# Moving the copy of a state's upper part behind the next step's gates in a gated graph network

## The reference

```python
A = (adj != 0)
for l in range(5):
    m = einsum('bnd,de->bne', h, weight[l])
    agg = einsum('bij,bid->bjd', A, m)
    gi = agg @ w_ih.T + b_ih;  gh = h @ w_hh.T + b_hh
    r = sigmoid(i_r + h_r);  z = sigmoid(i_z + h_z)
    n = tanh(i_n + r * h_n)
    h = (1 - z) * n + z * h
```

## Time and profile before

| | |
|---|---|
| median of 3 runs | 735.71 us |
| the profiled execution | 734.84 us |
| its span, first to last instruction | 733.0 us |
| TensorE busy | 684.8 us, 93% |
| VectorE busy | 564.6 us, 77% |
| ScalarE busy | 541.5 us, 74% |
| GpSimd busy | 300.4 us, 41% |
| mean granted TensorE clock | 0.994 |

### The profile page before, as it was taken

One profiled execution on the slowest core, in us unless ns is written; L12 is line 12 of the kernel. 1 busy time (PEld: TensorE's weight loads), 2 busy tenths in 40 slices (PEclk: granted clock), 3 DMA queues, 4 the chain that ended last, 5 costly groups with the idle time before them and its releaser, 6 DMA issues.

```text
span 733.0 us, 12659 instructions
## 1 busy us (share of the span) xinstructions
PE 684.8 (93%) x4226; PEld 587.3 (80%) x4226; DVE 564.6 (77%) x1362; ACT 541.5 (74%) x1167; POOL 300.4 (41%) x427
## 2 busy tenths in 40 slices
PE   3999899989999989989999999989999998989986
PEld 2787788879888779878978868879878887978766
DVE  4689986888978886789988886798886786787334
ACT  5577788668788878667878978657888768647653
POOL 4322435464335443573244534573334225642412
PEclk9999999999999999999999999999999999999999
DMA  6520011200000020410000020110000000110001
GB/s 162 126 80 1 2 30 32 58 1 4 6 4 1 1 61 2 130 44 2 5 7 1 2 61 1 59 59 2 6 6 1 1 1 1 58 58 5 9 1 58
DMA packets 47624, 21.10 MB, mean 29 GB/s; under 512 B 9032, under 2 KB 47560, under 8 KB 47560
## 3 DMA queue, kind: packets, MB, share of 16 engines
q1 hardware_dynamic: 47560, 20.29, 10.3%
HBM read 15.27 MB, written 4.19 MB: 27 GB/s over the span
## 4 chain that ended last, share of the span: by engine, by line
PE 55%; DVE 19%; ACT 14%; issue 6%; POOL 4%; DMA 1%; DVEq 0%; SPq 0%; POOLq 0%; ACTq 0%
PE bank L404 9%; PE bank L406 9%; PE bank L405 9%; PE bank L399 6%; DVE rh L1353 3%; PE bank L390 3%; ACT x_in L704 2%; ACT xn L704 2%; DVE bank L1356 2%; PE bank L592 2%; PE bank L604 2%; PE bank L607 2%; POOL rstd L945 2%; ACT rh L901 2%; PE bank L555 2%
## 5 line engine op out<-in xcount | busy, mean ns | idle before, releaser
L961 POOL TENSOR_TENSOR h_lo<-h,h_hi 128x512 fp32r<-128x512 f32 x64 | 82.6, 1291 | 243.2 <-ACT h_hi L876 243.2
L1353 DVE SCALAR_TENSOR_TENSOR rh<-bank,rh 128x512 f32<-128x512 f32 x80 | 55.0, 688 | 87.0 <-ACT bank L909 86.9
L404 PE MATMUL bank<-h_hi,whh_hi 128*128 128x512 f32 x240 | 105.8, 441 | 12.9 <-DVE rh L1353 11.9
L404 PE MATMUL bank<-g_hi,wc_hi 128*128 128x512 f32 x240 | 102.6, 427 | 0.0
L406 PE MATMUL bank<-h_lo,whh_hi 128*128 128x512 f32 x240 | 95.0, 396 | 0.0
L405 PE MATMUL bank<-h_hi,whh_lo 128*128 128x512 f32 x240 | 94.5, 394 | 0.0
L406 PE MATMUL bank<-g_lo,wc_hi 128*128 128x512 f32 x240 | 94.4, 393 | 0.0
L405 PE MATMUL bank<-g_hi,wc_lo 128*128 128x512 f32 x240 | 93.7, 391 | 0.0
L399 PEld LDWEIGHTS bank<-edge,hn 128*128 128x128 f32 x640 | 83.6, 191 | 8.4 <-DVE edge L1061 2.0
L915 ACT ACTIVATE bank<-bank,bih 128x512 f32<-128x512 f32 x80 | 52.9, 661 | 45.2 <-DVE bank L1356 45.1
L399 PE MATMUL bank<-edge,hn 128*128 128x128 f32 x640 | 84.3, 274 | 1.6 <-DVE edge L1061 1.6
(11 more groups left out here) (168 smaller groups left out, 1668.1 us busy)
## 6 DMA issues: line engine op xcount, KB each, us to landing
x_in<-in_x SPq DMA_DIRECT2D x8, 512.0 KB, 5.4
adj_in<-in_adj SPq DMA_DIRECT2D x8, 512.0 KB, 5.0
x_res<-in_x SPq DMA_DIRECT2D x16, 256.0 KB, 2.8
out_x<-x_res SPq DMA_DIRECT2D x16, 256.0 KB, 2.3
xz<-x_res SPq DMA_DIRECT2D x16, 50.0 KB
w_sb<-in_L_gnn_W SPq DMA_DIRECT2D x1, 640.0 KB, 5.2
w_sb<-in_L_gnn_W SPq DMA_DIRECT2D x5, 128.0 KB, 5.1
rows<-in_adj SPq DMA_DIRECT2D x32, 0.6 KB
```

The source lines that it names most:

```text
L404: nc.tensor.matmul(dst[:], w_hi, m_hi, start=start, stop=False)
L961: nc.gpsimd.tensor_tensor(h_lo[q][:], h[q][:], h_hi[q][:].bitcast(f32), ALU.subtract).then_inc(sem["h_lo_new"], 1)
L1353: nc.vector.scalar_tensor_tensor(rh[:], R_BANK[:], 1.0, rh[:], ALU.add, ALU.mult).then_inc(sem["rh_ready"], 1)
```

## The change

ScalarE's call of `split_new(n - 1)` moves from ahead of the tanh of r to behind the copy to `g_hi`, right ahead of the tanh of n. GpSimd calls `beside(2n)` ahead of `low_half(n - 1)` instead of behind it; `beside(2n + 1)` stays behind. No instruction is added or removed, and the streams of TensorE, VectorE and SyncE are the same.

```diff
@@ scalar
                 beside(2 * n)
-                if n and (n - 1) % STEPS < SPLITS:
-                    split_new(n - 1)
                 act.wait_ge(sem["gates_r"], n + 1)
                 nc.scalar.activation(R_BANK[:], R_BANK[:], ACT.Tanh, bias=brz[:, 0:1], scale=0.5).then_inc(sem["r_ready"], 1)
                 act.wait_ge(sem["gates_z"], n + 1)
                 nc.scalar.activation(gz[n % 2][:], Z_BANK[:], ACT.Tanh, bias=brz[:, 1:2], scale=0.5).then_inc(sem["z_ready"], 1)
                 if n + 1 < ALL:
                     aggregate_hi(n + 1)
+                if n and (n - 1) % STEPS < SPLITS:
+                    split_new(n - 1)
                 act.wait_ge(sem["pre_ready"], n + 1)
@@ gpsimd
             for n in range(ALL + TAIL_STEPS):
+                beside(2 * n)
                 if n and n <= ALL and (n - 1) % STEPS < SPLITS:
                     low_half(n - 1)
-                beside(2 * n)
                 beside(2 * n + 1)
```

## The result

The changed kernel takes 736.7 us, the median of 12 runs (735.12 to 739.14), against 735.36 us for the kernel before in 12 runs. The ratio is 1.0023, with a 95% interval of 1.0012 to 1.0033. The forecast was 0.4% less time; it became 0.2% more. The profiled execution has a span of 734.4 us, 1.4 us more than before.

What follows compares the result with a forecast made beforehand. TensorE, busy 93% of the span, was taken as the bound. +3.0 (round 0) - 5.9 (gains) = -2.9 us took 734.84 to 731.9; the median's 0.87 made 732.8 us. Own range 730 to 735, over all cases 729 to 739.

Steps and rivals of the forecast that it cites:

- (a): Steps 24, 44, 64: gated no longer meets the low half, rh 0.88 us earlier, TensorE idle goes: 2.6 us gained.
- (b): Steps 32 to 34 and 52 to 54: blocks lose 1.0 us, products come 1.4 us earlier; two rounds, 2.8 us.
- (c): Step 74: TensorE's wait of 1.44 us at 606.08 shrinks by 0.5 us.
- The race for zh: Light steps: low half starts 0.04 us before zh, which ends 1.1 us later; the other order's bound is 0.4 us.
- Round 0: Early-step zh delays, a later tanh of n, and normT and adjacency waits: 1.7 + 0.2 + 1.15 = +3.0 us.
- where VectorE is over 1.3 us late it escapes: Steps with VectorE over 1.3 us late: zh was to avoid the low half, taken to end at 2.48 us.
- the clock: TensorE's slow stretch behind idles at 54.57 and 85.98: one more or fewer, 0 in sum, 1.7 us each way.
- Only where VectorE is the last to arrive: Later zh was to cost time only in round 0's early steps, where VectorE arrives last.
- the loop through h: Rival, steps 32 to 36 of each round: h's loop grows up to 1.1 us a step; 741 us, chance 0.20.
- the written signs: If right: gated, mix, blocks never above 0.75 us, hardly any tanh-of-n idle; if wrong: xn of steps 33 to 36 waits longer.
- handed on: Rival: idle removed returns at the next wait for L901, half of 5.9 us goes; 735.7 us, chance 0.28.
- zh did not win its race: Rival: zh starts first in light steps, h loses 0.4 us, round 0 costs 1.5; 731.3 us, chance 0.07.

Runs made afterwards that it cites:

- e2: Kernel before with only GpSimd's even side work moved ahead of the low half, ScalarE's copy left early: 736.4 us, ratio 1.0004.
- e1: Changed kernel with GpSimd's order of before (low half ahead of even side work), ScalarE's copy late: 773.9 us, ratio 1.0503.
- e4: Changed kernel (copy late) with GpSimd's low half one step later, waiting for VectorE's rh: 725.5 us, ratio 0.9846.
- e3: Changed order of ScalarE and GpSimd from step 21 on only, round 0 as in the kernel before: 730.4 us, ratio 0.9917.
- e7: Changed kernel with GpSimd's low half also waiting for g_lo, so it starts just behind zh's start: 727.1 us, ratio 0.9883.
- e5: Kernel before (copy early) with only GpSimd's low half moved, one step later and behind rh: 726.9 us, ratio 0.9877.

## Why the prediction was wrong

**The gains, right.** (a) rh ahead of step 25's products was to come 0.88 us earlier; from step 24 to step 26 the products gain 0.89, 0.88 and 0.83 us in the three rounds. (b) 1.4 us a round was forecast, 1.7 and 1.3 measured. (c) 0.5 forecast, 0.5 measured. Small waits that were not seen took some back. L477 waits 0.3 us for diff in steps 23, 43 and 63; with the 0.28 us gained one step ahead that is some +0.15 us a round. Step 73 adds 0.25. In place of -5.9 the three rounds gave -5.2, less 0.7 lost to a stretch at half clock in step 40 of this execution.

**The race for zh, right.** zh under the low half, its end 0.54 us behind it, the 1.1 us of a light step, and gated, mix and blocks free in steps 24 and 31 to 33: all as written. "GpSimd winning by 0.04 us" is the margin that the trace has in the light steps.

**Round 0, the term that failed.** "Round 0: 1.7 + 0.2 + 1.15 = +3.0 us" came out as +5.9 (0.25 of it the start). The miss lies ahead of the products of step 10, on VectorE's chain from step 3 on:

| term | forecast | measured |
|---|---|---|
| zh of step 3 and b_share | +2.1 | +2.1 |
| blocks no longer caught | -0.95 | -0.9 |
| half clock at 58.49: g_lo of step 5 waits | 0 | +0.85 |
| zh of step 5, less a wait of 0.8 that it fills | 0 | +0.3 |
| zh of step 6 | +1.0 | +1.1 |
| zh of steps 7 and 8 | 0 | +1.0 |
| rowsI | -0.45 | -0.4 |
| rh ahead of the products of step 10 | +1.7 | +4.2 (4.50 less the 0.26 of the start) |

The rows above the last add up to 4.05; a further 0.1 us is a wait ahead of L1356 in step 5, the rest rounding.

A miss of 1.0 us is one that the forecast had ruled out: "where VectorE is over 1.3 us late it escapes". In steps 7 and 8 VectorE is about that late (zh starts 2.50 and 2.30 us after g_hi, against 1.24 in a light step), but so is GpSimd: the low half ends 3.12 and 2.95 us after g_hi starts, and not the 2.48 of the forecast. By GpSimd's own move, put at "Nothing late, I take 0", the norm goes ahead of the low half. Step 8:

```profile
81.23 0.60 ACT L880 ACTIVATE g_hi<-bank 128x512 fp32r<-128x512 f32 x1 [0.45 <-PE bank L399]
...
81.64 1.01 POOL L945 TENSOR_TENSOR rstd<-var_eps,neg_half 128x4 f32<-128x4 f32 x1
...
82.88 1.30 POOL L961 TENSOR_TENSOR h_lo<-h,h_hi 128x512 fp32r<-128x512 f32 x1
83.53 1.19 DVE L1329 SCALAR_TENSOR_TENSOR zh<-gz,h 128x512 f32<-128x512 f32 x1
```

e2 has the same 1.18 us in both steps without the copy's move. e1, without GpSimd's, confirms it for step 7, where zh is back at 0.68 us, but not for step 8: there VectorE is less late, and zh takes 1.37. A miss of nearly the same size is the clock. The idle of 2.46 us at 56.95 was followed by a stretch at the lower level, 1.2 GHz, and the one of 2.36 us at 90.47 was not, where before had it. Granted clock is the number behind the busy times:

```profile
58.49:61.90 3.41, 3.41 (x12) 0.50 0.03 5
90.40:94.90 4.50, 4.43 (x23) 1.00 0.00 0
```

The forecast had said that the stretch could come or go, and put 0. In VectorE's chain it is +0.85. e1 shows the price apart from the rest: it has the same idle at the same place and no such stretch behind it, and its products of step 6 come 1.4 us earlier than those of the changed kernel (1.42 us after before's, not 2.86):

```profile
56.89 0.51 PE L404 MATMUL bank<-h_hi,whh_hi 128*128 128x512 f32 x1 [2.46 <-DVE rh L1353]
...
58.49:61.90 3.41, 3.41 (x23) 1.00 0.03 5
```

The 1.4 us that come back behind step 10 pay for three losses further on: 0.7 in steps 10 to 13 (forecast 0.2, and 0.15 for the adjacency), 0.94 at the two L362, which was right (0.48 and 0.62 us of wait in place of nothing and 0.18), and 1.1 behind step 16. There three VectorE instructions (zh, h and edge) are caught one after the other, by three of GpSimd's:

```profile
137.64 1.29 POOL L961 TENSOR_TENSOR h_lo<-h,h_hi 128x512 fp32r<-128x512 f32 x1 [1.48 <-ACT h_hi L876]
137.68 1.79 DVE L1329 SCALAR_TENSOR_TENSOR zh<-gz,h 128x512 f32<-128x512 f32 x1
138.88 1.74 POOL L973 TENSOR_TENSOR adjTI<-adjT,ident 128x512 f32<-128x512 f32 x1
...
140.10 1.07 DVE L1342 SCALAR_TENSOR_TENSOR h<-zh,hd 128x512 f32<-128x512 f32 x1
140.77 1.31 POOL L996 TENSOR_TENSOR adjT<-adjT,norm 128x512 f32<-128x512 f32 x1
141.10 1.26 DVE L1061 TENSOR_SCALAR edge<-adj_in 128x512 f32<-128x512 f32 x1
```

**"Only where VectorE is the last to arrive", too narrow.** The forecast charged zh to round 0 alone and took the loop through h for a rival that needs 0.5 us a step to decide. It never became the bound, but it did eat: freed of the low half, steps 30 to 34, and their like 20 and 40 steps on, gain 1.4, 1.4 and 1.1 us more (e4), 4 us together. No row of before had shown that, for in these steps zh met no low half there.

**The signs.** Three of the written signs went the other way. The tanh of n keeps 20.2 of its 45.2 us of idle. gated still takes 1.47 us in step 21 and 1.46 in step 61 (1.45 and 1.44 before), under a low half of a round's first states, which did not move. And the sign that was to speak for the loop through h came: xn of steps 33 and 34 waits 2.83 and 1.17 us for the shift, after 2.36 and 0.35. From xn to xn it is now 8.88 us and not 8.58, which is the growth of 0.3 a step that the rival had worked out, and under the 0.5 from which it decides: the products of the steps 34 to 37 all come 3.5 us late, so nothing is lost there.

**The rivals.** The gains were not handed on (e3: rounds 1 to 3 are 5.3 us shorter). That this rival's 735.7 us lies nearer to the result than the forecast's 732.8 is luck: round 0 took the gains. The loop did not become the bound. zh did not win its race; where it is made to, in e7, the kernel takes 727.1 us and not the 731.3 of that rival.

## What to carry to other kernels

When an instruction moves, follow what waits for it to its new place and list what runs on the neighbour engine there: here the low half's place was worth four to six times the copy's (1.2% in e5 by the ratio, or 8.5 us by the medians, against 0.3% or 1.4 us from e5 to e4). Give a helper's work a start that is tied to the engine it can collide with (here, behind rh, beside instructions that read a bank), rather than to its input. And where two engines start within 0.1 us of each other, the price of either order is part of the range, in every step that has the pair.

## What the runs showed of the hardware

The order of starts decides who waits. The Trainium skill, "SBUF — State Buffer", section "Who interferes with whom", says that issue order and not the kind of operation decides. The changed kernel and e7 agree, with zh at 1.79 and 0.68 us and the low half at 1.29 and 1.66. In the 57 steps of the changed kernel in which the low half starts ahead of zh, by 0.04 to 1.06 us, zh ends 0.54 to 0.56 us after it each time.

Not only instructions with two SBUF operands of full size are caught. edge reads one (0.41 us alone in step 16 before, 1.26 in its row under "Why the prediction was wrong"), and so does blocks of the earlier trace rows, whose second operand is one number for each partition: 1.25 us then and 0.35 now. The same section says that a copy or tensor_scalar in a two-port mode takes part in the contention; the durations agree, and no run here shows the mode itself.

An idle of about the same length was followed by a stretch at the lower clock level in one execution and not in another. One pair is the 2.46 us ahead of step 5's products in the changed kernel and in e1 (granted 0.50 and 1.00 behind it). Another is 1.34 us in step 40 of before (granted 1.00 from 318 to 325 us), 1.35 us in step 40 of the changed kernel, then 3.41 us at 0.50:

```profile
324.73:328.14 3.41, 3.41 (x14) 0.50 0.02 6
```
